# The shortest chunk's maxima tiles mixed with the next group's longest, one sum step moved, the MLP loops written out with a split end, and two first loads put into the last group

## The reference

```python
mod = silu(condition) @ Wada + bada            # six rows of 512 per batch entry
sh_a, sc_a, gt_a, sh_m, sc_m, gt_m = split(mod, 6)
xm = layernorm(x, g1, be1) * (1 + sc_a) + sh_a
q, k, v = split(xm @ Wqkv)                     # 16 heads
p = softmax(where(causal, q @ k.T * 32**-0.5, -inf))
x = x + gt_a * ((p @ v) @ Wproj + bproj)
xm = layernorm(x, g2, be2) * (1 + sc_m) + sh_m
x = x + gt_m * (gelu(xm @ W1 + b1) @ W2 + b2)
```

## Time and profile before

| what | value |
|---|---|
| median of three runs | 2236.59 us (2233.2 to 2237.03) |
| the profiled execution | 2236.31 us, its span 2234.1 us |
| PE busy | 2154.2 us, 96% of the span |
| POOL, DVE, ACT busy | 965.7, 1286.7, 929.2 us |
| phase a | 0 to about 347 us |
| phase b | about 347 to 1398 us |
| phase c, projection | 1399 to 1514 us |
| phase c, MLP | 1514 to 2234 us |

### The profile page before, as it was taken

One profiled execution on the slowest core, in us unless ns is written; L12 is line 12 of the kernel. 1 busy time (PEld: TensorE's weight loads), 2 busy tenths in 40 slices (PEclk: granted clock), 3 DMA queues, 4 the chain that ended last, 5 costly groups with the idle time before them and its releaser, 6 DMA issues. The chain is left out here.

```text
span 2234.1 us, 31272 instructions
## 1 busy us (share of the span) xinstructions
PE 2154.2 (96%) x11326; PEld 1443.9 (65%) x11326; DVE 1286.7 (58%) x2872; ACT 929.2 (42%) x1780; POOL 965.7 (43%) x380
## 2 busy tenths in 40 slices
PE   6999999999999999999999999899999999999998
PEld 5888885454444545454444544677888888888886
DVE  4778876777777777777777754784313213133132
ACT  2111115566566656655655665335322222222221
POOL 2001007979799797988979773760000000000000
PEclk9999999999999999999999999999999999999999
DMA  6548346235261522625243222784101011011010
GB/s 235 206 151 266 127 168 158 63 76 120 54 138 46 119 66 63 149 49 131 52 112 80 59 77 63 247 319 155 67 37 57 0 56 56 0 56 56 0 38 19
DMA packets 129240, 222.96 MB, mean 100 GB/s; under 512 B 8526, under 2 KB 26006, under 8 KB 128920
## 3 DMA queue, kind: packets, MB, share of 16 engines
q1 hardware_dynamic: 107992, 179.38, 29.5%
q10 hardware_dynamic: 21120, 41.95, 5.1%
HBM read 146.31 MB, written 74.98 MB: 99 GB/s over the span
## 5 line engine op out<-in xcount | busy, mean ns | idle before, releaser
L1170 ACT ACTIVATE prob<-st 128x512 f32<-128x512 f32 (+3 forms) x1280 | 608.0, 542 | 387.2 <-PE st L1344 371.6
L1140 POOL TENSOR_TENSOR psum_k<-psum_k,prob 128x2048 f32<-128x2048 f32 (+1 forms) x150 | 670.8, 4472 | 21.0 <-ACT prob L1170 5.4
L1226 DVE TENSOR_REDUCE part<-mx 128x1 f32<-128x512 f32 x702 | 459.0, 685 | 107.0 <-PE mx L1324 104.0
L1344 PE MATMUL st<-q_st,k_st 98*128 98x512 f32 (+3 forms) x1280 | 489.8, 395 | 8.1 <-ACT prob L1170 4.1
L1324 PE MATMUL mx<-k_st,qx_st 96*128 96x512 f32 (+3 forms) x1189 | 465.7, 407 | 17.7 <-DVE part L1222 5.6
L1738 DVE TENSOR_TENSOR m_g_lo<-m_g,m_g_hi 128x512 fp32r<-128x512 f32 x128 | 88.6, 693 | 494.8 <-ACT m_g_hi L1652 494.8
L1344 PEld LDWEIGHTS st<-q_st,k_st 98*128 98x128 f32 x1280 | 242.7, 190 | 194.3 <-issue 103.1
L1324 PEld LDWEIGHTS mx<-k_st,qx_st 96*128 96x128 f32 x1189 | 224.0, 190 | 169.7 <-DVE part L1226 107.3
L1222 DVE CUSTOM_DVE_ANT_0 unused<-mx,mask_row 128x256 bf16<-128x256 f32 x487 | 230.6, 485 | 124.8 <-PE mx L1324 119.7
L1361 PE MATMUL o_ps<-prob,v_sb 128*32 128x512 f32 (+3 forms) x2560 | 285.6, 551 | 3.0 <-POOL prob L1123 3.0
L1648 ACT ACTIVATE m_g<-m_hid,vcol 128x512 f32<-128x512 f32 x128 | 88.2, 689 | 480.3 <-PE m_hid L1835 480.3
(11 more groups left out here) (168 smaller groups left out, 2593.5 us busy)
## 6 DMA issues: line engine op xcount, KB each, us to landing
k_st<-qk_scratch SPq DMA_DIRECT2D x96, 256.0 KB, 8.3
qx_st<-qk_scratch SPq DMA_DIRECT2D x96, 256.0 KB, 5.0
q_st<-qk_scratch SPq DMA_DIRECT2D x96, 256.0 KB
qk_scratch<-st_hi ACTq DMA_DIRECT2D x16, 1024.0 KB, 4.2
qk_scratch<-st_lo ACTq DMA_DIRECT2D x16, 1024.0 KB, 6.9
xs<-in_x_dram SPq DMA_DIRECT2D x8, 1024.0 KB, 8.7
v_sb<-v_scratch SPq DMA_DIRECT2D x8, 1024.0 KB, 15.4
o_scratch<-o_sb SPq DMA_DIRECT2D x32, 256.0 KB, 2.3
```

The costliest lines, as they stand in the source:

```text
L1140: nc.gpsimd.tensor_tensor(dst, src, prob[:, s % BUF, :, m:], ALU.add).then_inc(pool_added, 1)
L1170: nc.scalar.activation(prob[:, s % BUF, h, m:], st[n % RING][:, m:], ACT.Exp, scale=SCALE).then_inc(exp_done, 1)
L1226: nc.vector.tensor_reduce(most, bank[:, 0:w], AX.X, ALU.max).then_inc(mx_free, 1)
L1344: nc.tensor.matmul(st[n % RING][:, m:], k_st[u][0:MROWS, h, kt * P:(kt + 1) * P], q_st[0:MROWS, pos % 2, h, m:], start=True, stop=True).th ...
```

## The change

Four things change.

1. **Items.** `work` was: the items of `pos` 1, 2, 3, then the next group's `pos` 0. Now `pos` 3 (16 items, all on the diagonal, 128 to 512 wide) and the next group's `pos` 0 (64 items) form one list: three of `pos` 0, one of `pos` 3, sixteen times, then the last 16 of `pos` 0. In a group without the last, blocks 1 to 6 and 16 to 20 keep their items. Blocks 7 to 15 had 11, 8, 6, 9, 10, 9, 9, 7, 6 and have 10, 7, 6, 10, 10, 10, 9, 7, 6. DVE gets a wait at each chunk's first item for an older maximum of its own.
2. **One sum step.** In the chunk of 16 steps step 13 is now added by POOL (384 wide) and step 11 is multiplied by PE (512 wide).
3. **First loads.** x of chunk 0 and the attention's output of chunk 1 are loaded by SP in the last group instead of at the start of phase c, into buffers placed anew.
4. **MLP.** All loops are written out. PE no longer waits for its own last sums at a chunk's end, `finish`'s additions of the bias move to tiles 8 to 11, `gated` has two halves, and in the last chunk PE multiplies the last three hidden tiles by token rows (12 multiplications of tile 12 first, then nine for each 128 tokens); the output of that chunk is stored in four parts.

```diff
-    POOLED = {3: (0, 1, 2, 3, 4, 5, 6, 8, 9, 10, 11, 12), 2: (0, 1, 2, 3, 4, 5, 6, 8, 9), ...}
+    POOLED = {3: (0, 1, 2, 3, 4, 5, 6, 8, 9, 10, 12, 13), 2: (0, 1, 2, 3, 4, 5, 6, 8, 9), ...}
...
+        longest, shortest = self.batch[0], self.batch[QC - 1]
+        share = len(longest) // len(shortest)
+        mixed = []
+        for n, it in enumerate(shortest):
+            mixed += longest[(share - 1) * n:(share - 1) * (n + 1)] + [it]
+        end = len(mixed)
+        mixed += longest[(share - 1) * len(shortest):]
+        mixed.insert(end + LATER, QC - 1)
         work = []
-        for pos in (*range(1, QC), 0):
-            start = len(work)
-            work += self.batch[pos]
-            work.insert(start + LATER, (pos or QC) - 1)
+        for pos, found in ((1, self.batch[1]), (2, self.batch[2]), (QC - 1, mixed)):
+            work += [*found[:LATER], pos - 1, *found[LATER:]]
...
+                else:
+                    sp.wait_ge(p_ready, BATCH)
+                    sp.dma_start(E.x0[:, :, :], x[0:CH, :]...).then_inc(K.x0_loaded, 16)
+                    steps_done(g, 2)
+                    sp.dma_start(E.o_in[1][:, :, :], K.o[0:KT, :, CH:2 * CH]...).then_inc(K.o1_loaded, 16)
                 store_o(g, 2)
...
+                if it is L.batch[pos][0] and QC * g + pos >= 2:
+                    dve.wait_ge(mcol_ready, QC * g + pos - 1)
...
-            load_o(1)
-            load_x(0)
             load_x(1)
             load_o(2)
...
-            with nc.sync.Fori(0, NCH - 1) as n:
-                body(n, True)
-            body(NCH - 1, False)
+            for n in range(NCH - 1):
+                ...
+            n = NCH - 1
+            for s in range(TT):
+                sp.wait_ge(out_ready, TT * n + s + 1)
+                sp.dma_start(out[n * CH + s * P:n * CH + (s + 1) * P, :], ms[:, s, :]).then_inc(out_stored, 16)
...
-                if n >= 2:
-                    pool.wait_ge(xn_ready, TT * max(n - OB + 1, 1))
+                if n >= OB:
+                    pool.wait_ge(xn_ready, TT * (n - OB + 1))
...
+            for n in range(1, NCH):
                 for j in range(HT):
                     tile(n, j)
+                    if j >= HT - 2 * TT and j < HT - TT:
+                        add_bias(n, j - HT + 2 * TT)
...
-                else:
-                    pe.wait_ge(sum_ready, TT * (n + 1))
-                    pe.sem_inc(used, 1)
...
-            with nc.tensor.Fori(1, NCH) as n:
+            for n in range(1, NCH - 1):
                 for j in range(HT + LAG):
                     ...
+            n = NCH - 1
+            for j in range(HT):
+                hidden(n, j)
+                if LAG <= j < HT - 2:
+                    multiply(n, j - LAG)
+            multiply(n, HT - 4)
+            for s in range(TT):
+                for j in range(HT - 3, HT):
+                    multiply_tokens(n, j, s)
```

More of the change, by code:

```diff
@@ L109, in __init__ @@
         self.p_hi, self.p_lo, self.o_hi, self.o_lo, self.p_raw = at[0:4:2], at[1:4:2], at[4], at[5], at[6]
-        at = over(*((n, [P, KT, D], F32) for n in ("under_p_hi0", "p_full0", "under_p_hi1", "p_full1", "under_o_hi0", "o_in0")))
-        self.p_full, self.o_in = at[1:4:2], at[5]
+        at = over(*((n, [P, KT, D], F32) for n in ("under_p_hi0", "p_full0", "under_p_hi1", "p_full1", "under_o_hi0", "o_in0", "x0", "o_in1")))
+        self.p_full, self.o_in, self.x0 = at[1:4:2], [at[5], at[7]], at[6]
         self.k_st = sb("k_st0", [P, GH, SEQ], F32R)
@@ L1180, in first_o_high @@
                 for t in range(KT):
-                    nc.scalar.activation(E.o_hi[:, t, :], E.o_in[:, t, :], ACT.Copy).then_inc(o_hi_ready, 1)
+                    nc.scalar.activation(E.o_hi[:, t, :], E.o_in[0][:, t, :], ACT.Copy).then_inc(o_hi_ready, 1)
             def copy(g, pos):
@@ L1451, in phase_project_mlp @@
         g32 = sb("m_g32", [P, 2, CH])
[L1452 removed]
+        gated = sb("m_gated", [P, 2, D])
         bst = sb("p_bst", [P, TT, 6])
@@ L1689, in _ @@
             xm_high(1, xr)
-            with nc.scalar.Fori(1, NCH - 1) as n:
+            for n in range(1, NCH):
                 for j in range(HT):
                     tile(n, j)
-                act.wait_ge(xm_loaded, 16 * (n + 1))
-                xm_high(n + 1, xr)
-            for j in range(HT):
-                tile(NCH - 1, j)
+                if n < NCH - 1:
+                    act.wait_ge(xm_loaded, 16 * (n + 1))
+                    xm_high(n + 1, xr)
         @block.vector
@@ L1788, in _ @@
             xm_low(1, xr)
-            finish(0, K.gate[:, 1, 0, :], gbias[:, 0, :])
-            with nc.vector.Fori(1, NCH - 1) as n:
+            for s in range(TT):
+                add_bias(0, s)
+            finish(0)
+            for n in range(1, NCH):
                 for j in range(HT):
                     tile(n, j)
-                xm_low(n + 1, xr)
-                b = n // (NCH // BATCH)
-                finish(n, K.gate[:, 1, bass.ds(b, 1), :], gbias[:, bass.ds(b, 1), :])
-            for j in range(HT):
-                tile(NCH - 1, j)
-            finish(NCH - 1, K.gate[:, 1, BATCH - 1, :], gbias[:, BATCH - 1, :])
+                    if j >= HT - 2 * TT and j < HT - TT:
+                        add_bias(n, j - HT + 2 * TT)
+                if n < NCH - 1:
+                    xm_low(n + 1, xr)
+                finish(n)
         @block.tensor
         def _(pe):
-            pe.sem_inc(used, 4)
             def project(n, s):
```

126 lines of the change are left out of this document (68 added, 58 removed).

## The result

| | before | after |
|---|---|---|
| median of six runs, us | 2236.81 (2233.2 to 2239.05) | 2244.63 (2242.51 to 2245.75) |
| ratio, 95% interval | | 1.0035 [1.0022, 1.0048] |
| the profiled execution: time, span | 2236.31, 2234.1 | 2245.05, 2243.0 |

The change made the kernel 0.35% slower. The forecast was 2231.5, and 2244.63 lies above the range (2219 to 2243). It lies on rival B, which had 15%.

A forecast was written before the change was run, and what follows sets the result against it. PE, busy for 2154.2 us, was taken to set the time. Attention +10.5, start of phase c -3.5, MLP loops -7.6 and the end -4.3 gave -4.9 us from 2236.31: forecast 2231.5, range 2219 to 2243.

The forecast's parts named there:

- rival B: Attention, block 7: the wait sets PE to half clock in each group, 1.8 us more per group, 2244 us; chance 0.15.
- the end: Behind PE's last multiplication: three of four token blocks finished and stored while PE still multiplies, 8.56 us becomes 4.3, -4.3 us.
- Part 1: Attention, block 7: late load of buffer 0 makes PE wait 3.1 us; with block 6's 0.86, +1.4 us per group.
- The clock behind the wait: Attention, behind the 3.1 us wait: PE may run at half clock, +0.6 us per group, bounds 0 and 1.8.
- Part 2: Attention sum step: step 13's wait for POOL goes, block 8 -0.3 us; items more even in blocks 9 to 15, -0.2.
- Part 3: Start of phase c: with first loads early, PE's 2.02 us wait goes and chunk 1's stages come 1.5 earlier, -3.5 us.
- Rival D: Start of phase c: the chain through x_scratch and o_in keeps its dates, -3.5 becomes 0, 2235 us; chance 0.14.
- Part 4: MLP: writing the loops out removes a 1.09 us surplus at the loop's edge in seven chunks, -7.6 us.
- A: Attention: the wait is covered by other gains or a shorter landing, attention comes out even, 2221 us; chance 0.13.
- A2: Attention: the load isn't late and mixing gives what it can, 2.2 us per group, 2206 us; chance 0.04.
- C: MLP: instructions arrive late in the written-out code, the 7.6 us come back inside the chunks, 2239 us; chance 0.06.

The follow-up runs named there:

- the kernel that kept PE at work: Changed kernel with 13 multiplications of 512 columns put before PE's wait for buffer 0, result unread: 2232.72 us, ratio 0.9979 against the kernel before.

## Why the prediction was wrong

By its own parts, in us of the profiled executions:

| part | forecast | measured |
|---|---|---|
| attention, seven groups | +10.5 | +27.1 |
| start of phase c | -3.5 | -7.5 |
| MLP loops | -7.6 | -7.6 |
| the end | -4.3 | -4.7 |
| elsewhere (end of phase a 1.5, last group 0.2, odds) | 0 | +1.6 |
| sum | -4.9 | +8.9 |

**Part 1, the wait.** Right in place and size. Full at 5.9 us behind the last item forecast, 6.1 measured; wait 3.1 forecast, 3.22 measured; block 6 +0.86. With the clock at 1.00, block 7 was forecast at 9.36: the four such blocks of the kernel that kept PE at work are 9.42 to 9.93.

**The clock behind the wait: here it failed.** "I take +0.6 (a third of 1.8), with bounds of 0 and 1.8." Three groups with the wait and the clock at 1.00 (windows of the kernel that kept PE at work):

```profile
481.57:614.49 132.92, 130.28 (x798) 67.13 (x794) 98.28 (x252) 78.56 (x164) 111.51 (x39) 1.00 0.40 89
...
887.76:1020.09 132.33, 130.33 (x798) 67.09 (x794) 98.27 (x252) 78.58 (x164) 111.48 (x39) 1.00 0.40 89
...
1153.86:1286.80 132.94, 130.44 (x798) 67.08 (x794) 98.36 (x252) 78.73 (x164) 111.48 (x39) 1.00 0.40 89
```

Their mean is 132.73, 0.65 above the 132.08 of before (forecast without the clock: 0.9). The changed kernel's mean is 135.95. So the half clock costs 3.2 us per group, five times what I took. Of this 2.0 lie in block 7 (11.70 against 9.68 in these three groups), 0.3 in block 8, 0.8 in block 17, and the rest in the first group's first blocks. Blocks 7 and 8 alone, 2.3 us right behind the wait, are outside my bound of 1.8. That block 17's part comes from the wait isn't shown: with the old item list and no wait, block 17 was long in six of seven groups.

The account of a group: 131.1 (before at full clock), -1.4 sum step, +3.0 wait and mixed order (132.73 - 129.75), +3.2 half clock = 135.9; before stood at 132.08, since it had 0.9 of half clock itself. So against the kernel before the half clock grew by 2.3.

The reasoning failed in two steps. I took the length of the half-clock stretch (3.3 us) from one instance; it covered more here, about 10 us in the fifth group: the items and all products of block 7. (Half of 3.3 is 1.65, too, and not the 1.8 that I wrote.) And I held that "as items are paced by DVE, only part shows"; but the products aren't paced by DVE, and they doubled (3.22 against 1.71). Two idle stretches with two outcomes are no reason for a third of the price when the wait comes in every group. The Trainium skill ("TensorE: Matmul & The Clock Gate", section "HAM oscillation — how this bites in real kernels") said that each repetition would start cold. The trace agrees: block 7's granted clock was 0.60 to 0.74 in all seven groups.

**Part 2.** POOL's wait went: no product in block 7 waits for a select any more. At full clock the step is a gain of 1.4 us a group. The spreading of items over blocks 9 to 15 was costed at -0.2, and that is what it gave. Windows over these blocks in the fifth group, both at full clock, of the kernel that kept PE at work and of the one with the old item list:

```profile
950.26:994.62 44.36, 44.06 (x260) 22.11 (x256) 34.74 (x89) 27.80 (x57) 43.49 (x14) 1.00 0.15 35
```

```profile
933.40:977.94 44.54, 44.05 (x258) 21.73 (x254) 35.02 (x76) 28.13 (x57) 43.24 (x14) 1.00 0.17 41
```

Only the order whose mixing starts behind eight items costs 0.7 in a group.

**Part 3.** The mechanism was right and the size half of what came: -7.5 measured against -3.5, outside my bound of -5. The loads alone give 6.9. The chain's transfers of 10 us stayed (10.18 and 10.81), but the first began 5.4 us earlier behind PE's start, and I had let only 1.5 of it through. Rival D, whose ground was these transfers, falls.

**Part 4 and the end** are right in size. For the loops the reason was half right: with the loops written out 0.6 of the 1.09 us stayed, at PE's wait for its own sums. So of the 1.09 that I put down to the loop's edge alone, only 0.5 us per chunk is its own.

A and A2 fall with the measured wait, C with chunks of 87.04. B had the right mechanism, but its total is right by luck. It put its 1.8 on top of the 0.6 already in the forecast; with 1.8 in its place it would have been 2239.8. And two errors nearly cancelled: phase c gained 4.4 more than I forecast, and the attention lost more than B had. Its sign, a clock in block 7 below 0.65 in most groups, came in three of seven only, since the window holds the wait, most of which is at full clock.

## What to carry over

- When a reordering makes an instruction the first reader of a reused buffer, compute when the refill can be issued (last reader's end) and landed, before counting any gain from the order. Here 6.1 us had to be covered, and eight items of the other buffer with block 6's last products did it.
- A wait of 3 us on PE in every repetition is to be priced twice: once as idle, once as work at half clock behind it (here 3.0 and at least 2.3 us a group). Bound the second by the whole work up to where the next full-clock stretch begins, not by a share of it.
- The kernel with the old item list and the rest of the change (0.9916 [0.9899, 0.9934] and 0.9937 [0.9912, 0.9961]) beats both kernels: the phase-c parts were worth 20 us and were hidden by one line of the planner.

## What the runs showed of the hardware

The half clock isn't tied to visible idle time. In the kernel with the old item list blocks 13 and 17 fell to 0.78 in some groups and not in others, with the same instructions and no wait: 6.20 against 7.80 us. With work added there, both kept their clock, and block 7 was long in six groups instead of three; whether the one caused the other isn't shown. The half clock can also hide which of two kernels is better: two that differ by one sum step came out 6 us apart one way and 7 us the other. Where stretches fall in some groups and not in others, a gain of 1 us a group has to be read from groups at clock 1.00, not from the total.
